# Writing out the middle-block loop of four attention layers, with fixed addresses, in a one-core Trainium2 kernel

## The chip, the cores and the metric

The kernel runs on one core of a Trainium2 chip (trn2). The core has five engines that work side by side, each with its own stream of instructions: TensorE (PE, with its weight loads PEld), VectorE (DVE), ScalarE (ACT), GpSimd (POOL) and SyncE (SP), which here only issues transfers. They meet through semaphores: an instruction may wait until a counter has reached a value, and may raise one when it is done. The metric is the device time of one execution in microseconds (us), lower is better.

## The reference, cut to what matters

A float32 network of four layers; each layer is an attention-like step and a feed-forward step, each followed by a residual sum and a layer norm:

```python
x = _layernorm(x + _L0_attn_ref(x, ...))   # x is (4, 512, 128)
x = _layernorm(x + _L0_ffn_ref(x, ...))
x = _layernorm(x + _L1_attn_ref(x, ...))   # 16 heads of 8, not causal
x = _layernorm(x + _L1_ffn_ref(x, ...))    # mixture of 8 experts, and a shared one
x = _layernorm(x + _L2_attn_ref(x, ...))   # 16 heads, causal, rotary
x = _layernorm(x + _L2_ffn_ref(x, ...))    # grouped-query attention, then 8 experts
x = _layernorm(x + _L3_attn_ref(x, ...))   # grouped-query, causal, with a bias by distance
x = _layernorm(x + _L3_ffn_ref(x, ...))
```

Four of these steps hold a softmax attention over 512 positions and 16 heads of width 8. All four are run by one piece of the kernel, with L = 0 for `_L1_attn_ref`, L = 1 for `_L2_attn_ref`, L = 2 for the attention in `_L2_ffn_ref` and L = 3 for `_L3_attn_ref`. In each:

```python
scores = einsum(q, k) * scale           # per head 512 x 512
attn = softmax(where(mask, -inf, scores))
out = einsum(attn, v) @ wo.T
```

## The kernel before, in words

The batch of four sequences is four **blocks** b = 0..3 of 512 tokens. An attention layer takes them in order, and in each block four **groups** g = 0..3 of four heads. One pass over (b, g) is a **unit**, so a layer has 16 units and a block four. In a unit every engine does its own share, written as a function `unit(L, b, g)` in each engine's program:

- PE: in 10 to 16 items i, `score_t` (L1606, with the mask by L1608) forms the transposed scores of this unit, and `score` (L1590, L1593) forms the plain scores of the unit two ahead, whose row maxima are needed; `values` (L1620) multiplies the exponentials by V; `shift_t` (L1631) and `o_t` (L1640) are small transposes.
- ACT: `PT` (L912) is the exponential of each `score_t` bank.
- DVE: the row maxima, by `TENSOR_REDUCE` (L1189) or, for wide causal tiles, by an addition of the mask with a running maximum (L1186).
- POOL: splits the maxima into bfloat16 parts (L706 to L712), and does the square roots of the norms (L619, L621) and parts of the split of Q and K (L684, L687).
- SP: stores the parts of Q and K (`store_parts`, L511 on), loads the stacks of a group (`load_stack`, L525 and L529) and the shift rows (`load_shift`, L536).

Work of other blocks is laid into the units at fixed places. In g = 0 of block b the projections of block b + 1 are made (`prep_pe` L1574 and L1570, `prep_act`, `prep_pool`). In g = 0 to 3 the block before is ended: its output projection in g = 1 (`y_out`, L1510), its norm in g = 1 and 2 on DVE (`post_sum`, `post_norm` L1026, `stats` L1006 and L1009), and its transpose in g = 3. Nothing reorders any of this: the order is the order in which the program is written, engine by engine.

`sequence` decides which of it is a loop. Block 0 and block 3 are written out; blocks 1 and 2 are one loop body of four units, run twice, on each of the five engines:

```python
def sequence(L, unit, Fori):
    for g in range(NG):
        unit(L, 0, g)
    with Fori(1, NB - 1) as b:
        for g in range(NG):
            unit(L, b, g)
    for g in range(NG):
        unit(L, NB - 1, g)
```

In the body b is a register. A semaphore's threshold that depends on b has to be computed in a register by the engine's sequencer (the rows at L226, L1179, L910 and others), and some helpers add a semaphore increment beside such a wait (L591 on POOL, L1185 on DVE, `pe_passed` on PE). A block's place in `XT` (the transposed input) is also computed from b. For the projection of the values, XT stands on the stationary side of the matmul, and there the body uses a copy at a fixed place, `XTS`: ACT copies XT of the next block to it (L855, `xts`, at item 0 of g = 0), and the projection at L1570 reads XTS and waits for that copy. Where b is a plain number, `prep_act` returns at once for `xts`, and L1570 reads XT itself.

Of the kernel before, what the change touches and what calls it, by code (L numbers as in the profile page):

```python
# [28 lines left out]
NB = 4  # L29
# [5 lines left out]
NG = H // GH  # L35
# [193 lines left out]
def build(nc, d):  # L229
    ctx = ExitStack()  # L230
    with ctx:
# [189 lines left out]

        def sequence(L, unit, Fori):

            for g in range(NG):
                unit(L, 0, g)
            with Fori(1, NB - 1) as b:
                for g in range(NG):
                    unit(L, b, g)
            for g in range(NG):
                unit(L, NB - 1, g)  # L430

# [21 lines left out]
        def ends_chain(L):  # L453
            return any(L == c[-1] for c in CHAINS)
# [16 lines left out]
        def _(sp):  # L471
# [67 lines left out]
            def attention_sp(L):  # L539
# [14 lines left out]
                def unit(L, b, g):  # L554
# [8 lines left out]
                    elif g >= 2 and ahead:  # L563
                        load_stack(ahead[0], ahead[1], g - 1)
                sequence(L, unit, sp.Fori)

            attention_sp(0)
            attention_sp(1)

# [13 lines left out]
        def _(pool):  # L583
            g = nc.gpsimd
# [136 lines left out]
            def attention_pool(L):  # L721
# [5 lines left out]
                def unit(L, b, gg):  # L727
# [14 lines left out]
                    if ahead:  # L742
                        shift(*ahead)
                sequence(L, unit, pool.Fori)

# [50 lines left out]
        def _(act):  # L796
# [100 lines left out]
            def attention_act(L):  # L897
# [6 lines left out]
                def unit(L, b, g):  # L904
                    u = U(L, b, g)
                    prev, follow, ahead, prep, end = neighbours(L, b, g)
                    for i, (kt, js) in enumerate(ST_ITEMS[L]):
# [18 lines left out]
                        if L in GATED_BY and is_last(b) and (g, i) == (2, GATES_AT):  # L926
                            gate_exp(GATED_BY[L], 0)
                sequence(L, unit, act.Fori)
                if ends_chain(L):
                    o_out(L, U(L, NB - 1, NG - 1), NG - 1)  # L930

            def gate_exp(p, part):

                act.wait_ge(gm_ready, gate_part(p, part) + 1)
                t = gate_tiles(part)
                a.activation(GE[:, t, :], GL[:, t, :], ACT.Exp).then_inc(ge_ready, 1)
# [64 lines left out]
        def _(dve):  # L1001
# [200 lines left out]
            def attention_dve(L):  # L1202
# [16 lines left out]
                def unit(L, b, g):  # L1219
                    u = U(L, b, g)  # L1220
                    prev, follow, ahead, prep, end = neighbours(L, b, g)
                    for i in range(NI[L]):
# [24 lines left out]
                        if L in GATED_BY and is_last(b):  # L1247
                            if (g, i) == (2, GATES_AT):
                                gates(GATED_BY[L], 0)
                            if GATED_BY[L] == L1_MOE and g == 3 and i in GATES_T_AT:  # L1250
                                gates_out(GATED_BY[L], GATES_T_AT[i], bank[0])
                                gates_out(GATED_BY[L], GATES_T_AT[i], bank[1], True)
                sequence(L, unit, dve.Fori)
                if ends_chain(L):
# [70 lines left out]
            def gates_out(p, b, src, parts=False):  # L1325

                gi = 0 if p == L1_MOE else 1
                dve.wait_ge(gt_ready, (gi * NB + b) * 2 + (2 if parts else 1))
                if parts:
                    v.tensor_copy(blk(RWT, b)[0:PARTS * NGATE, :], src[0:PARTS * NGATE, 0:T // 2].bitcast(BF16)).then_inc(gt_evac, 1)  # L1330
                else:
                    v.tensor_copy(blk(RW9, b), src[0:NGATE, :]).then_inc(gt_evac, 1)
# [158 lines left out]
        def _(pe):  # L1491
# [158 lines left out]
            def attention_pe(L):  # L1650
# [23 lines left out]
                def unit(L, b, g):  # L1674
                    u = U(L, b, g)
                    prev, follow, ahead, prep, end = neighbours(L, b, g)
                    for i in range(NI[L]):
# [27 lines left out]
                        if L in GATED_BY and is_last(b):  # L1705
                            if g == 2 and i in LOGITS_AT:
                                logits(GATED_BY[L], LOGITS_AT[i], bank[5])
                            if GATED_BY[L] == L1_MOE and g == 3 and i in GATES_T_AT:
                                gates_t(GATED_BY[L], GATES_T_AT[i], bank[0])
                                gates_t(GATED_BY[L], GATES_T_AT[i], bank[1], True)  # L1710
                sequence(L, unit, pe.Fori)
                if ends_chain(L):
# [282 lines left out]
```

## Time and profile before

| what | us |
|---|---|
| median of 3 runs | 1387.44 |
| lowest and highest of the 3 | 1387.06, 1394.69 |
| the profiled execution | 1386.62 |
| its span (first to last instruction) | 1384.8 |
| PE busy in the span | 1218.0 (88%) |
| DVE busy | 932.8 (67%) |
| ACT busy | 710.5 (51%) |
| POOL busy | 269.9 (19%) |

The profile is of one execution; what lies around its span is 1.8 us. In its 40 slices PE is busy at 0.8 or more in nearly all of the stretch from 130 us on. The attention layers are at about 136 to 360 us (L = 0), 564 to 930 us (L = 1 and 2, one after the other) and 1136 to 1315 us (L = 3). TensorE's granted clock is at its full level in the loop blocks. Where a time of a block or unit is given, it is from the start of the first L1606 matmul of one to that of the next.

### The profile page before, as it was taken

The page shows a single profiled execution, that of the slowest core. Times are in us where ns is not written, and L with a number is a line of the kernel's source. Part 1 is how long each engine was busy: PE and PEld are TensorE (multiplying, and loading weights), DVE is VectorE, ACT ScalarE, POOL GpSimd, SP SyncE. Part 2 cuts the span into 40 slices and gives each one's busy share as a digit, 9 for nine tenths or more (in the row PEclk, how much of TensorE's full clock was granted, in tenths as well). Part 3 has the DMA queues.
Part 4 walks back from the last instruction along what each step waited for, and adds up shares of the span by engine and source line. Part 5 has one row for each costly group of instructions (what it writes and reads, how often), then busy time and mean ns, then how long its engine had stood idle before and what let it go on. Part 6 is the DMA issues. An engine that isn't in the chain of part 4 may idle for free.

```text
span 1384.8 us, 26785 instructions
## 1 busy us (share of the span) xinstructions
PE 1218.0 (88%) x8190; PEld 650.1 (47%) x8190; DVE 932.8 (67%) x2502; ACT 710.5 (51%) x1300; POOL 269.9 (19%) x557
## 2 busy tenths in 40 slices
PE   3446999999889998999999999999999979999876
PEld 1222233333356655445555555556666535455445
DVE  5877778687455555767778776755554476668676
ACT  2221776777644434566666666663222227666643
POOL 3342211111000012322332332110000211222112
PEclk7557999999999998999999999999999989999988
DMA  7312232310000003323333222100000202221000
GB/s 207 124 65 73 87 90 68 120 35 19 1 1 1 0 1 120 105 66 107 106 98 126 74 78 76 45 4 3 1 0 0 74 12 67 77 81 40 2 1 31
DMA packets 65200, 79.16 MB, mean 57 GB/s; under 512 B 5483, under 2 KB 58068, under 8 KB 64602
## 3 DMA queue, kind: packets, MB, share of 16 engines
q1 hardware_dynamic: 65098, 77.89, 18.1%
q8 instruction: 52, 0.85, 0.3%
q14 instruction: 50, 0.41, 0.1%
HBM read 45.27 MB, written 31.72 MB: 56 GB/s over the span
## 4 chain that ended last, share of the span: by engine, by line
PE 62%; issue 13%; DVE 9%; ACT 4%; DMA 4%; DVEq 3%; POOL 2%; SPq 1%; POOLq 1%; ACTq 0%
PE bank L1606 11%; PE bank L1620 11%; PE bank L1590 9%; PE bank L1772 6%; PE bank L1773 6%; PE bank L1790 5%; PE bank L1574 3%; PE bank L1608 2%; DVE M L1189 2%; DMA KS<-scr_k 2%; PE bank L1640 2%; DVE masked_scores L1186 1%; PE bank L1510 1%; DVE N L1026 1%; PE bank L1570 1%
## 5 line engine op out<-in xcount | busy, mean ns | idle before, releaser
L912 ACT ACTIVATE PT<-bank 128x512 f32<-128x512 f32 (+1 forms) x784 | 427.5, 569 | 246.9 <-PE bank L1608 176.2
L1590 PE MATMUL bank<-KS,QS 125*128 125x512 bf16 (+3 forms) x1024 | 308.6, 329 | 31.5 <-DVE M L1186 12.1
L1606 PE MATMUL bank<-QS,KS 128*128 128x512 bf16 (+3 forms) x1024 | 303.7, 323 | 15.2 <-ACT PT L912 8.0
L1189 DVE TENSOR_REDUCE M<-bank 128x1 f32<-128x512 f32 (+2 forms) x400 | 257.8, 684 | 87.9 <-PE bank L1590 52.2
L1186 DVE CUSTOM_DVE_ANT_0 masked_scores<-bank,maskw 128x384 bf16<-128x384 f32 (+1 forms) x384 | 228.7, 622 | 90.0 <-PE bank L1590 78.8
L1620 PE MATMUL bank<-PT,VA 128*32 128x512 f32 (+3 forms) x2048 | 211.5, 485 | 1.6 <-ACT PT L912 1.0
L1606 PEld LDWEIGHTS bank<-QS,KS 128*128 128x128 bf16 x1024 | 99.3, 98 | 215.5 <-ACT PT L912 152.4
L1590 PEld LDWEIGHTS bank<-KS,QS 125*128 125x128 bf16 x1024 | 100.6, 99 | 109.0 <-DVE M L1189 31.9
L1608 PE MATMUL bank<-identb,maskw 128*128 128x128 bf16 x768 | 147.7, 219 | 0.0
L1790 PEld LDWEIGHTS bank<-MW,PT 128*128 128x128 f32 x864 | 111.7, 193 | 40.8 <-issue 38.2
L1772 PE MATMUL bank<-XT,MW 128*128 128x512 f32 (+1 forms) x232 | 120.7, 602 | 10.1 <-DVE PT L1363 5.9
L1773 PE MATMUL bank<-XT,MW 128*128 128x512 f32 (+1 forms) x232 | 119.4, 596 | 0.0
L1790 PE MATMUL bank<-MW,PT 128*128 128x128 f32 x864 | 112.2, 276 | 1.2 <-DVE PT L1363 1.2
L953 ACT ACTIVATE PT<-bank 128x512 f32<-128x512 f32 x64 | 38.2, 597 | 130.0 <-PE bank L1773 130.0
L1365 DVE TENSOR_TENSOR PT<-bank,PT 128x512 f32<-128x512 f32 x64 | 44.2, 691 | 79.9 <-ACT PT L953 78.6
L1608 PEld LDWEIGHTS bank<-identb,maskw 128*128 128x128 bf16 x768 | 75.3, 98 | 21.4 <-issue 7.0
L706 POOL CAST MS<-M 128x16 bf16<-128x16 f32 x64 | 12.7, 198 | 331.4 <-DVE M L1189 331.4
L1773 PEld LDWEIGHTS bank<-XT,MW 128*128 128x128 f32 x232 | 44.2, 191 | 55.5 <-issue 55.5
L1504 PE MATMUL bank<-ident,N 128*128 128x128 f32 x128 | 24.8, 328 | 50.5 <-DVE N L1026 50.5
L1620 PEld LDWEIGHTS bank<-PT,VA 128*32 128x32 f32 x2048 | 40.3, 108 | 60.2 <-issue 22.6
L1593 PE MATMUL bank<-maskw,identb 128*128 128x128 bf16 x384 | 66.1, 223 | 0.0
L1359 DVE SCALAR_TENSOR_TENSOR PT<-bank,CC,PT 128x512 f32<-128x512 f32 x52 | 39.0, 749 | 37.3 <-ACT PT L948 37.0
(229 smaller groups left out, 1522.6 us busy)
## 6 DMA issues: line engine op xcount, KB each, us to landing
scr_q<-PQ SPq DMA_DIRECT2D x48, 384.0 KB, 3.2
QS<-scr_q SPq DMA_DIRECT2D x64, 288.0 KB
scr_k<-PK SPq DMA_DIRECT2D x24, 384.0 KB, 3.6
KS<-scr_k SPq DMA_DIRECT2D x32, 288.0 KB
QS<-MSB SPq DMA_DIRECT2D x192, 4.0 KB
MW<-in_m_w SPq DMA_DIRECT2D x3, 1024.0 KB, 9.5
MW<-in_m_w SPq DMA_DIRECT2D x3, 832.0 KB
scr_k<-PK SPq DMA_DIRECT2D x24, 96.0 KB, 1.9
```

What stands on the lines that cost most here:

```text
L912: a.activation(PT[kt % 2][:, js[0]:js[-1] + 1, q0:T], tiles(bank[st_bank(L, g, i)][:, 0:w * len(js)], len(js)), ACT.Exp, scale=c["scale"]) ...
L1186: v.tensor_tensor_reduce(masked_scores[S_ORDER[L][i]][:, 0:kl], bank[S_ORDER[L][i]][:, 0:kl], maskw[:, T - kl:T], -1.0, FLT_MAX, ALU.add, ...
L1189: v.tensor_reduce(M[g % 2][:, t * GH + js[0]:t * GH + js[-1] + 1], tiles(bank[S_ORDER[L][i]][:, 0:kl * len(js)], len(js)), AX_X, ALU.max, ...
L1365: v.tensor_tensor(H1[c % NH1[p]], bank[2 + c % 2][:, :], A1[c % 2], ALU.mult).then_inc(h_ready, 1)
L1590: r = mm(s, QS[0:ROWS_SHIFT, g * GH + j, t * P:(t + 1) * P], KS[0:ROWS_SHIFT, kv_slot(L, g, j), 0:kl], start=True, stop=not by_pe)
L1593: r = mm(s[:, kl - P:kl], identb[:, :], maskb[:, :], start=False, stop=True)
L1606: r = mm(s, KS[:, kv_slot(L, g, j), kt * P:(kt + 1) * P], QS[:, g * GH + j, T - w:T], start=True, stop=not causal)
L1608: r = mm(s[:, 0:P], maskb[:, :], identb[:, :], start=False, stop=True)
L1620: r = mm(bank[4][32 * j:32 * (j + 1), q0:T], VA[:, kt, kv_slot(L, g, j), :], PT[kt % 2][:, j, q0:T], start=(kt == 0), stop=(kt == NT - 1))
L1772: mm(bank[c % 2][:, :], MW1[:, c * P:(c + 1) * P], blk(XT, b), start=True, stop=True)
L1773: r = mm(bank[2 + c % 2][:, :], MW3[:, c * P:(c + 1) * P], blk(XT, b), start=True, stop=True)
L1790: r = mm(to[:, i * P:(i + 1) * P], H1[c % NH1[p]][:, i * P:(i + 1) * P], MW2[:, c, :], start=(starts and i == 0), stop=stops, skip_group_c ...
```

## The change

`sequence` no longer takes a loop; it writes all 16 units out, with b a plain number everywhere. The five calls lose their last argument. The rest of the text is as it was, so lines after this place stand 4 lower in the new kernel. By the rules above the register arithmetic, the branches and the extra increments of the body are no longer issued, the copy to XTS is not made, and the projection at L1570 reads XT. The body of four units stands twice in each engine's stream.

```diff
-        def sequence(L, unit, Fori):
-
-            for g in range(NG):
-                unit(L, 0, g)
-            with Fori(1, NB - 1) as b:
+        def sequence(L, unit):
+
+            for b in range(NB):
                 for g in range(NG):
                     unit(L, b, g)
-            for g in range(NG):
-                unit(L, NB - 1, g)
...
-                sequence(L, unit, sp.Fori)
+                sequence(L, unit)
...
-                sequence(L, unit, pool.Fori)
+                sequence(L, unit)
...
-                sequence(L, unit, act.Fori)
+                sequence(L, unit)
...
-                sequence(L, unit, dve.Fori)
+                sequence(L, unit)
...
-                sequence(L, unit, pe.Fori)
+                sequence(L, unit)
```

First place, ACT at the start of the body of L = 0 (block 1, g = 0). PT0 and PT1 are the exponentials, PQ and QF the two copies of the projected Q, REGISTER_ALU and the bare ISA rows are register work. Before:

```order
L912 ACTIVATE PT1<-bank3 128x512
L426 UNCONDITIONAL_BRANCH
L426 ISA
L226 ISA
L912 ACTIVATE PT0<-bank2 128x512
L853 ISA
L226 REGISTER_ALU
L855 ISA
L855 ACTIVATE XTS<-XT 128x512
L910 REGISTER_ALU
L912 ACTIVATE PT0<-bank3 128x512
```

The same place in the changed kernel:

```order
L908 ACTIVATE PT1<-bank3 128x512
L908 ACTIVATE PT0<-bank2 128x512
L908 ACTIVATE PT0<-bank3 128x512
L866 ACTIVATE PQ<-bank6 128x512
L867 ACTIVATE QF<-bank6 128x512
L908 ACTIVATE PT0<-bank2 128x512
```

The exponentials and the two copies of Q keep their order; the copy to XTS and the register rows between them are gone.

Second place, DVE in g = 2 of the body of L = 1, where the norm of the block before stands between the row maxima of the unit two ahead (masked_scores, M). Before:

```order
L1006 BN_STATS ST<-N 128x6 x4
L1009 BN_AGGR MV<-ST 128x2 x4
L1018 TENSOR_TENSOR MS<-MV 128x4
L1020 TENSOR_TENSOR MS<-MS,MV 128x4
L1179 REGISTER_ALU
L1186 ISA masked_scores,M<-bank,maskw 128x384
L1186 ISA M 128x1
L1179 REGISTER_ALU
L1186 ISA masked_scores,M<-bank,maskw 128x384
L1186 ISA M 128x1
```

In the changed kernel:

```order
L1002 BN_STATS ST<-N 128x6 x4
L1005 BN_AGGR MV<-ST 128x2 x4
L1014 TENSOR_TENSOR MS<-MV 128x4
L1016 TENSOR_TENSOR MS<-MS,MV 128x4
L1182 ISA masked_scores,M<-bank,maskw 128x384
L1182 ISA M 128x1
L1182 ISA masked_scores,M<-bank,maskw 128x384
L1182 ISA M 128x1
```

The work is in the same order; the register rows ahead of each maximum are gone.

## Rows read from the trace of the kernel before

**Rows 1.** The page, busy time, share and count of each engine.

```profile
PE 1218.0 (88%) x8190; PEld 650.1 (47%) x8190; DVE 932.8 (67%) x2502; ACT 710.5 (51%) x1300; POOL 269.9 (19%) x557
```

**Rows 2.** Busy time by stretch; loop blocks 1 and 2 of L = 0, 1, 2, 3.

```profile
core 0: us, PE busy (x) PEld busy (x) DVE busy (x) ACT busy (x) POOL busy (x), PEclk, DMA share, GB/s
192.61:312.53 119.92, 114.55 (x632) 38.56 (x633) 90.88 (x173) 86.92 (x165) 21.68 (x54) 1.00 0.25 80
609.17:706.47 97.30, 92.01 (x836) 50.82 (x833) 72.84 (x233) 61.47 (x120) 28.73 (x62) 1.00 0.32 100
800.36:892.43 92.07, 91.86 (x836) 49.70 (x832) 68.41 (x207) 61.13 (x120) 25.84 (x58) 1.00 0.21 66
1179.99:1275.21 95.22, 89.27 (x828) 48.51 (x824) 68.18 (x225) 62.60 (x122) 24.76 (x58) 1.00 0.20 64
```

**Rows 3.** Semaphore and register work that each engine issues at L226.

```profile
L226 PEldq ALU_OP  x642: 32/32/36, 192.8 to 1273.2; - x161
```

**Rows 4.** By stretch, L = 1: g = 2 of block 2, then of block 3.

```profile
685.07:696.29 11.22, 10.05 (x96) 5.25 (x97) 9.80 (x36) 6.63 (x13) 3.14 (x9) 1.00 0.20 54
732.85:743.57 10.72, 9.92 (x101) 5.27 (x97) 9.69 (x36) 6.64 (x13) 2.97 (x9) 1.00 0.12 38
```

**Rows 5.** DVE in time, L = 1, g = 2: block 1 (644 us), block 3 (740 us).

```profile
644.35 0.16 DVE L1020 TENSOR_TENSOR MS<-MS,MV 128x4 f32<-128x4 f32 x1
644.61 0.56 DVE L1186 CUSTOM_DVE_ANT_0 masked_scores<-bank,maskw 128x384 bf16<-128x384 f32 x1
...
740.05 0.16 DVE L1020 TENSOR_TENSOR MS<-MS,MV 128x4 f32<-128x4 f32 x1
740.13 0.55 DVE L1186 CUSTOM_DVE_ANT_0 masked_scores<-bank,maskw 128x384 bf16<-128x384 f32 x1
```

**Rows 6.** PE in time, L = 1, g = 2 of block 2: idle before, and releaser.

```profile
693.48 0.28 PE L1590 MATMUL bank<-KS,QS 125*128 125x256 bf16 x1 [1.17 <-DVE M L1186]
```

**Rows 7.** By stretch, g = 2 of block 1 of L = 3.

```profile
1206.39:1217.52 11.13, 10.20 (x101) 5.21 (x97) 10.05 (x36) 6.63 (x13) 3.65 (x9) 1.00 0.12 36
```

**Rows 8.** By stretch, L = 1: g = 1 of block 2, then of block 3.

```profile
673.96:685.07 11.11, 10.79 (x108) 6.30 (x105) 8.74 (x32) 7.27 (x15) 3.16 (x7) 1.00 0.48 160
722.12:732.85 10.73, 10.73 (x109) 6.27 (x105) 8.79 (x32) 6.86 (x14) 2.58 (x7) 1.00 0.24 65
```

**Rows 9.** By stretch, L = 0: g = 1 of block 1, then of block 3.

```profile
211.00:225.85 14.85, 14.28 (x80) 5.01 (x81) 12.42 (x29) 9.71 (x19) 2.06 (x6) 1.00 0.15 42
326.66:341.33 14.67, 14.22 (x81) 4.75 (x81) 12.32 (x29) 9.71 (x19) 2.05 (x6) 1.00 0.00 1
```

**Rows 10.** By stretch, L = 3, g = 0: block 1, then block 0.

```profile
1179.99:1195.67 15.68, 13.64 (x116) 7.03 (x113) 7.70 (x23) 10.72 (x21) 5.63 (x9) 1.00 0.32 107
1136.28:1150.67 14.39, 12.27 (x96) 5.98 (x96) 7.34 (x21) 9.59 (x18) 5.57 (x9) 1.00 0.30 98
```

**Rows 11.** The copy to XTS at L855, all 8; duration in ns.

```profile
L855 ACT ACTIVATE XTS<-XT x8: 621/621/622, 193.6 to 1228.8; 128x512 f32 x8
```

**Rows 12.** ACT in time, L = 3, block 1, g = 0.

```profile
1181.06 0.62 ACT L855 ACTIVATE XTS<-XT 128x512 f32 x1
1182.02 0.60 ACT L912 ACTIVATE PT<-bank 128x512 f32<-128x512 f32 x1 [0.33 <-PE bank L1608]
```

**Rows 13.** PE in time: g = 0 of block 1 of L = 3 and of L = 1.

```profile
1183.91 0.59 PE L1574 MATMUL bank<-XT,WC 128*32 x1 [0.77 <-ACT QF L871]
...
610.59 0.39 PE L1590 MATMUL bank<-KS,QS 125*128 125x512 bf16 x1 [0.97 <-DMA KS<-scr_k]
```

**Rows 14.** By stretch, L = 0: block 1, then block 2.

```profile
192.61:252.53 59.92, 57.27 (x317) 19.26 (x317) 45.40 (x87) 43.42 (x83) 10.84 (x27) 1.00 0.26 81
252.53:312.53 60.00, 57.27 (x316) 19.30 (x317) 45.49 (x87) 43.51 (x83) 10.84 (x27) 1.00 0.25 79
```

**Rows 15.** DMA queues of 192.6 to 252.5 us: packets, MB, share of 16 engines.

```profile
q1 hardware_dynamic: 4128, 4.77, 25.1%
q8 instruction: 3, 0.05, 0.3%
q14 instruction: 5, 0.04, 0.2%
```

**Rows 16.** DMA queues of 252.5 to 312.5 us, all of them.

```profile
q1 hardware_dynamic: 4128, 4.77, 25.2%
```

**Rows 17.** Branches of the loops on PE; duration in ns.

```profile
L426 PEldq COMPARE_BRANCH  x8: 76/148/227, 251.6 to 1274.1; - x8
```

## The prediction, made before the changed kernel ran

> **What bounds the kernel now.** I read the busy times first: PE is busy 88% of the span [rows 1], so it is the engine to follow, and only stretches in which PE stands idle can pay. Next I cut the span by blocks of the attention layers, since the change touches blocks 1 and 2 of each and nothing else. The reader is to subtract PE's busy time from each stretch [rows 2]: 119.92 - 114.55 = 5.37 us in L = 0, 97.30 - 92.01 = 5.29 in L = 1, 92.07 - 91.86 = 0.21 in L = 2, and 95.22 - 89.27 = 5.95 in L = 3. That is 16.82 us of idle PE in the 404.5 us that the loops take. PE's matmuls are the same in number and shape after the change, so this is all that there is to win in them, 1.2% of the time. Last I compared units in the loop with the same unit written out: blocks 0 and 3 already are what blocks 1 and 2 become, in the same execution and at the same full clock. These twins carry the forecast.
>
> **The register work.** It is removed. On PE alone one line issues 642 register operations of 32 ns [rows 3], 20.5 us of the sequencer's time. It costs nothing as long as the sequencer runs ahead of the array: in L = 2, which has the same kind of body, PE stands idle for 0.21 us in 92 us [rows 2]. So the 20.5 us are cover, not path, and I take nothing for them. They cost where an engine has just been waited for and its next instruction needs a threshold first. The place where this is seen is DVE in g = 2 of L = 1. There the norm of the block before delays the row maxima, and PE waits for them, 1.17 us [rows 6]. In the loop the maximum starts 644.61 - 644.35 = 0.26 us after the last operation of the norm, in the written-out block 740.13 - 740.05 = 0.08 us [rows 5]. That is 0.18 us at one such place, and there are others like it ahead of it.
>
> What the unit gets from all of them is read from the twins:
>
> - L = 1, g = 2: 11.22 us in the loop, 10.72 written out, with idle PE 1.17 and 0.80 [rows 4]. Gain 0.50 us, twice: 1.0. Most of the wait stays, because it is the norm's own work.
> - L = 3, g = 2: 11.13 us with 0.93 idle [rows 7]. Its written-out blocks have no norm at this place or another one, so it has no twin. It is the same body with the same kind of wait as in L = 1, and I take the same 0.50, twice: 1.0. Bounds: nothing, and all of its idle time, 2 x 0.93 = 1.9.
> - L = 1, g = 1: 11.11 against 10.73 [rows 8]. Gain 0.38, twice: 0.8. Block 1 has more idle here than block 2, from the start of the layer, which the change does not touch; I take block 2's difference for both.
> - L = 0, g = 1: 14.85 against 14.67 [rows 9]. Gain 0.18, twice: 0.4.
> - L = 2: nothing, since PE does not wait [rows 2].
>
> **The g = 0 units and the copy.** The copy takes 0.62 us of ACT, eight times [rows 11], 5.0 us in all. In L = 3 it ends at 1181.06 + 0.62 = 1181.68, and ACT's next exponential starts at 1182.02 after 0.33 us of waiting for PE [rows 12]. The cover is PE's own work for that exponential; take it away and the copy would cost up to 0.62 us each, 5.0 us together. The values projection waits for the copy in name, but it comes five items later, when the copy has long been made. What holds PE in g = 0 is other work: in L = 3 the evacuation of Q by ACT (0.77 us), in L = 1 the landing of a stack (0.97 us) [rows 13]. Neither becomes shorter. The test of it is block 0 of L = 3, which has the same projections without the copy and without a loop: it has 14.39 - 12.27 = 2.12 us of idle PE, and loop block 1 has 15.68 - 13.64 = 2.04 [rows 10]. So the copy and the loop together cost nothing that can be seen there. Each g = 0 unit has a few handoffs between POOL, ACT and PE that lose a register operation or two; I take 0.1 us for each of the six units of L = 0, 1 and 3, together 0.6, between 0 and half the difference of a g = 2 unit. What is late next, if DVE and ACT come earlier, is the same transfer or the same evacuation.
>
> **The branches.** PE's take 76 to 227 ns [rows 17], eight in all. They run on the sequencer, ahead of the array: blocks 1 and 2 of L = 0, of which the first ends with the jump back, take 59.92 and 60.00 us [rows 14]. Nothing is taken for them.
>
> **What is added: code.** The body stands twice, and the second copy has to be fetched. The first pass through the body of L = 0 shows what this looks like: 3 packets of instructions on one queue and 5 on the other [rows 15]. On the second pass there are none [rows 16]. Their time is 0.3% of 16 engines over 59.9 us, 2.9 us, and 0.2%, 1.9 us. The pass that fetches takes 59.92 us and the pass that doesn't 60.00 [rows 14], with the same idle PE (2.65 and 2.73). So the fetch lies beside the work, and its price is zero. If that cover were gone, on PE's queue alone, four layers would pay 4 x 2.9 = 11.6 us; with the other queue's, 4 x 4.8 = 19.2.
>
> The Trainium skill (Runtime: NRT & Kernel Launch, instruction fetch mechanics) says that a taken branch whose target is not in the window that the engine holds forces a fetch of the target before execution can go on, and that kernels therefore prefer to be written out. The trace does not agree for this body: the second pass fetches nothing. By that rule the jump back would stall, and removing it would save at least one fetch in each of four layers; by the rows it saves nothing.
>
> **The sum.** 1.0 + 1.0 + 0.8 + 0.4 + 0.6 = 3.8 us. The profiled execution took 1386.62 us, its span of 1384.8 and 1.8 around it; after the change 1386.6 - 3.8 = 1382.8. The median of the runs is 0.8 above the profiled one, so the forecast is 1383.6 us, 0.3% faster. That is within the 1% that a measurement of this kernel can tell from no change.
>
> **The rivals.**
>
> 1. *Small gains, as summed.* 1383.6 us. Chance 0.60.
> 2. *The twins mislead.* Block 3 differs from blocks 1 and 2 in what follows it as well as in being written out, and an idle stretch that closes in one unit can open in the next. Then the register work is hidden everywhere and the time stays: 1387 us, between 1386 and 1388.5. For it: L = 2 and the g = 0 units of L = 3, where loop and written-out code have the same idle time [rows 2, 10]. Chance 0.22.
> 3. *The fetches of the second copy are exposed.* Engines stall at block 2 of each layer because their instructions are not there. It decides if an engine empties what it holds before the next packet lands. In full on both queues 1387.4 + 19.2 = 1406.6 us, slower by 1.4%. On PE's queue alone 1387.4 + 11.6 = 1399; in part some us, slower by less than 1%. For it: more instruction packets will be there, beside up to 25% of DMA share [rows 15]. Against it: the fetching pass is not longer than the other. Chance 0.04 for over 1%, and 0.06 for less.
> 4. *The jump back stalls after all.* If each layer's jump costs PE one fetch, 2.9 / 3 = 1 us, in a form that the stretches do not show, the gain is 4 us more: 1379.6 us. This is what the skill's rule would make of it. Against it: no packet and no idle time at the jump [rows 14, 16]. Chance 0.03.
> 5. *All idle time of the loops goes.* If one thing in the loop, such as POOL's or ACT's waits on registers, were behind every wait, PE would close all 16.8 us: 1387.4 - 16.8 = 1370.6 us, faster by 1.2%. Against it: written-out units keep 0.80 us in g = 2 of L = 1 and 2.12 in g = 0 of L = 3 [rows 4, 10]. Chance 0.05.
>
> **How the numbers follow.** The time is that of the first. Its own range is from no gain on L = 3 and g = 0 (1385.2) to the full idle time of the g = 2 units of L = 3 and twice the rest (about 1380). The range for 8 in 10 takes in the second rival and the fourth with some room for the 0.8 us between median and profile: 1378.5 to 1388.5. The third and fifth, in all 0.15, stand mostly outside. Faster by over 1% is rival 5, 0.05; slower by over 1% is 3 in full, 0.04; within 1% is the rest, 0.91.
>
> **What would show each step.** In the profile after: the copy row is gone and the projection reads XT. Blocks 1 and 2 of L = 2 still take 46.0 us each. In L = 1 the g = 2 units take 10.7 us, with PE still waiting 0.8 us for DVE. The g = 0 units of L = 3 keep about 2 us of idle PE, waiting for the evacuation of Q and K. There are some 12 more packets of PE's instructions and no longer issue gaps beside them. The prediction is wrong if a block of L = 2 changes by over 0.5 us, since no wait of PE is there to be lost, or if idle PE appears at block 2 beside an instruction packet.

## The result, and the profile after

The changed kernel takes 1382.70 us in the median (1380.18 to 1387.88, 20 runs) against 1387.48 (1384.40 to 1394.69, 20 runs) for the kernel before: ratio 0.9969, with an interval of 0.9958 to 0.9979. The forecast was 1383.6. The profiled execution took 1381.19 us, with a span of 1379.4 against 1384.8, so the profile shows 5.4 us less.

Three parts of the page of the changed kernel: the engines (busy time, share, instructions, as [rows 1]) and the two queues that carry instructions (packets, MB, share of 16 engines).

```profile
PE 1200.9 (87%) x8105; PEld 647.8 (47%) x8190; DVE 932.1 (68%) x2502; ACT 705.8 (51%) x1292; POOL 268.3 (19%) x557
...
q8 instruction: 63, 1.03, 0.3%
q14 instruction: 54, 0.44, 0.1%
```

ACT has 8 instructions fewer: the copies to XTS are gone. The kernel before had 52 and 50 packets on the two queues, so 11 and 4 came with the second copies of the bodies. 85 matmuls have no record here (8105 of 8190), so PE's busy time reads low, and I compare lengths of stretches, not idle sums.

Busy time by stretch of the changed kernel: blocks 1 and 2 of L = 0, 1, 2, 3 (as [rows 2]), then single units, which are g = 1 of L = 0 [rows 9], g = 1 of block 2 [rows 8] and g = 2 of block 2 of L = 1 [rows 4], g = 2 of block 1 and g = 3 of block 2 of L = 2, g = 0 [rows 10] and g = 2 [rows 7] of block 1 of L = 3.

```profile
core 0: us, PE busy (x) PEld busy (x) DVE busy (x) ACT busy (x) POOL busy (x), PEclk, DMA share, GB/s
191.58:310.84 119.26, 112.75 (x620) 37.06 (x632) 90.47 (x173) 85.88 (x163) 21.60 (x54) 1.00 0.26 81
607.49:703.65 96.16, 90.13 (x828) 50.76 (x833) 72.57 (x233) 60.55 (x118) 28.64 (x62) 1.00 0.32 101
797.75:890.36 92.61, 90.20 (x828) 49.76 (x832) 68.10 (x207) 59.97 (x118) 25.49 (x58) 1.00 0.22 66
1176.07:1269.71 93.64, 87.49 (x820) 48.66 (x825) 68.15 (x225) 61.53 (x120) 24.68 (x58) 1.00 0.20 66
...
209.79:224.45 14.66, 14.16 (x79) 4.74 (x81) 12.30 (x29) 9.69 (x19) 2.05 (x6) 1.00 0.16 42
671.15:682.72 11.57, 10.63 (x107) 6.27 (x105) 9.20 (x32) 7.12 (x15) 3.13 (x9) 1.00 0.46 157
682.72:693.42 10.70, 9.68 (x95) 5.26 (x96) 9.26 (x35) 6.63 (x13) 2.91 (x8) 1.00 0.20 56
823.48:833.22 9.74, 9.58 (x99) 5.30 (x96) 8.26 (x27) 6.63 (x13) 1.13 (x6) 1.00 0.14 39
878.87:890.36 11.49, 10.19 (x103) 5.70 (x100) 7.13 (x22) 7.09 (x14) 1.04 (x5) 1.00 0.13 36
1176.07:1191.62 15.55, 13.49 (x115) 7.05 (x113) 7.79 (x23) 10.26 (x20) 5.62 (x9) 1.00 0.32 108
1202.34:1212.81 10.47, 9.76 (x99) 5.26 (x97) 9.52 (x35) 6.63 (x13) 3.63 (x9) 1.00 0.13 38
```

Against [rows 2] the loop blocks become 0.66, 1.14 and 1.58 us shorter in L = 0, 1 and 3, and 0.54 us longer in L = 2: together 2.8 us less, where 3.8 were forecast. The other 2.6 us of the span lie in places that the change does not touch; two steps hold most of it, 1.1 us ahead of the first attention and 1.7 us in the stretch from the last unit of L = 2 to L = 3 (210.5 us against 212.2 before). Experiment e12 shows that the second of these comes and goes with the execution.

What the register work did is seen where [rows 5] showed it. DVE of the changed kernel in time, L = 1, g = 2 of block 1:

```profile
641.25 0.16 DVE L1016 TENSOR_TENSOR MS<-MS,MV 128x4 f32<-128x4 f32 x1
641.33 0.55 DVE L1182 CUSTOM_DVE_ANT_0 masked_scores<-bank,maskw 128x384 bf16<-128x384 f32 x1
```

The maximum now starts 0.08 us after the last operation of the norm, as in the written-out block, instead of 0.26.

L = 2 holds two surprises. Its g = 2 units take 9.74 us instead of 10.13, where PE's row showed 0.11 us of idle time before. And g = 3 of block 2 takes 11.49 instead of 10.18, and has a wait that was not there. PE of the changed kernel in time, with its idle time and what ended it:

```profile
880.46 0.39 PE L1586 MATMUL bank<-KS,QS 125*128 125x512 bf16 x1 [1.14 <-DMA KS<-scr_k]
```

PE waits for a stack. Two rows of the DMA traffic of this kernel, from 877.9 to 879.3 us, show what was on the DMA engines while that stack came in (packets, MB, share of 16 engines):

```profile
q1 hardware_dynamic: 128, 0.11, 28.5%
q8 instruction: 1, 0.02, 5.1%
```

One packet of instructions, 0.02 MB, keeps one engine for 0.051 x 16 x 1.4 = 1.1 us. In the trace the semaphore of the stack has made all its steps but one by 879.15 us, and the last comes at 880.41, after the packet (878.02 to 879.17) has left its engine. The kernel before has no such packet there, because this is the second pass through a body whose code it does not fetch again; from 880 to 882.4 us it has only the data queue:

```profile
q1 hardware_dynamic: 364, 0.35, 45.7%
```

So three questions were open: what makes the g = 2 units shorter, and which engine; whether the copy costs anything; and whether the code packets are what takes a part of the gain back.

### The profile page after: what moved, and what is told of

Read it like the earlier page. It is cut to its first block, busy times and chain, and to the rows that moved or that the text cites. A ratio compares the mean times of both kernels' runs of the same rounds, so it can differ in the third digit from the quotient of the medians.

```text
span 1379.4 us, 24326 instructions
## 1 busy us (share of the span) xinstructions
PE 1200.9 (87%) x8105; PEld 647.8 (47%) x8190; DVE 932.1 (68%) x2502; ACT 705.8 (51%) x1292; POOL 268.3 (19%) x557
## 4 chain that ended last, share of the span: by engine, by line
PE 60%; issue 13%; DVE 10%; ACT 5%; DMA 4%; POOL 3%; DVEq 3%; SPq 1%; POOLq 1%; another core or an unknown queue 0%; ACTq 0%
PE bank L1616 10%; PE bank L1602 9%; PE bank L1586 9%; PE bank L1768 6%; PE bank L1769 6%; PE bank L1786 5%; PE bank L1570 3%; PE bank L1604 3%; DMA KS<-scr_k 2%; DVE masked_scores L1182 2%; DVE M L1185 2%; ACT PT L908 1%; PE bank L1636 1%; PE bank L1506 1%; DVE N L1022 1%
## 5 line engine op out<-in xcount | busy, mean ns | idle before, releaser
L1602 PE MATMUL bank<-QS,KS 128*128 128x256 bf16 (+1 forms) x953 | 276.4, 318 | 11.6 <-ACT PT L908 7.9
```

Of the source, the lines that this page charges most:

```text
L1602: r = mm(s, KS[:, kv_slot(L, g, j), kt * P:(kt + 1) * P], QS[:, g * GH + j, T - w:T], start=True, stop=not causal)
```

## The experiments

A unit is written (L, b, g) below. Three of the kernels are the same as another one: one profile has single waits that another does not repeat, and it has to be known which.

**The changed kernel again, twice.** No edit.

> The changed kernel once more, for a second profile of it. Theory A (what differs between the two profiles inside the attention layers comes from the change): the blocks 1 and 2 of L = 0, 1 and 3 take the same times as in the first profile within 0.1 us, and unit g = 3 of block 2 of L = 2 again takes 11.5 us with PE idle 1.1 to 1.3 us, because the packet of code at 878.0 us falls on the transfer of a stack at the same place of the program. Theory B (chance of one execution): that wait is gone or elsewhere, and the unit takes 10.2 us. Time about 1382.7 us under both, 0.3% under the kernel before.

> The changed kernel a third time, to be compared with the copy beside it on the same chip, and for a third profile. Theory A (the copy is free): this and the next run agree within 1 us in the median. The unit g = 3 of block 2 of L = 2 takes 11.0 to 11.6 us again, g = 0 of L = 1 15.6 to 16.2.

Measured: 1382.69 us beside 1390.05, ratio 0.9954 [0.9937, 0.9971], and 1385.85 beside 1388.97, ratio 0.9983 [0.9969, 0.9997]. Three timings of one pair of kernels thus give 0.9969, 0.9954 and 0.9983, further apart than each interval says; the second rests on 6 executions. Differences of 0.2% between two kernels can't be read from the times, and below I read units, which repeat. Blocks 1 and 2 are shorter than before by 3.1 us in the first (119.28 + 96.14 + 92.41 + 93.53 = 401.4 against 404.5) and 2.6 in the second. What repeats to 0.02 us in all three: (0, b, 0), (0, b, 1) and all g = 2 units. What does not: the units of L = 1 around the start of a block, and (2, 2, 3), with 11.49, 11.11 and 11.67 us. The wait behind the last, in the second repetition, PE in time:

```profile
884.44 0.39 PE L1586 MATMUL bank<-KS,QS 125*128 125x512 bf16 x1 [1.33 <-DMA KS<-scr_k]
```

**The copy put back, twice.** The changed kernel, but blocks 2 and 3 make and wait for the copy to XTS as in the loop.

```diff
-                if what == "xts" and isinstance(b, int):
+                if what == "xts" and isinstance(b, int) and b < 2:
...
-                    x = blk(XT, b) if isinstance(b, int) else XTS[:, :]
-                    if not isinstance(b, int):
+                    copied = not isinstance(b, int) or b >= 2
+                    x = XTS[:, :] if copied else blk(XT, b)
+                    if copied:
```

> The changed kernel, all written out, but with the copy to XTS for blocks 2 and 3 of each layer made on ACT and waited for by PE as in the kernel before. Theory A (the copy lies beside PE's work and costs nothing): the time of the changed kernel, within 0.5 us, and g = 0 of blocks 1 and 2 unchanged: 18.2 us in L = 0, 15.4 to 15.6 in L = 3. Rival (the copy was worth something): up to 8 x 0.62 = 5.0 us slower, which is all of the 4.8 us that the change gained.

> The changed kernel with the copy to XTS put back, the same kernel as the one with the copy above, since its median stood 2.7 us above the changed kernel's while its profile agreed with it in every unit. Theory A (the copy is free; the 2.7 us are the scatter of few runs): within 1 us of the changed kernel run beside it. Rival (the copy costs about what the change gained): again 2 to 5 us above it.

Measured: 1385.43 us, ratio 0.9972 [0.9956, 0.9987], and 1384.18 us, 0.9973 [0.9960, 0.9987]. (0, b, 0) takes 18.20 to 18.21 us in both, as without the copy; the g = 0 units of block 2 of L = 3 take 15.35 in both, again as without it. The copy lies beside PE's work, and its removal brings nothing that the units show. The medians alone would not tell: they lie 2.7 us above that of e1, timed beside the first, and 1.7 us under that of e11, timed beside the second, so both missed the margins that were expected (0.5 and 1 us), in opposite directions.

The two kernels are the same, so their profiles also show what differs between two executions. By stretch, from the last unit of L = 2 to L = 3, first of e2:

```profile
922.78:1133.32 210.54, 195.56 (x955) 120.39 (x952) 118.18 (x352) 58.29 (x96) 18.43 (x30) 0.98 0.05 14
```

and of e12:

```profile
924.29:1136.53 212.24, 197.59 (x955) 121.53 (x953) 118.28 (x352) 58.32 (x96) 18.44 (x30) 0.97 0.05 14
```

1.70 us more at a granted clock of 0.97 instead of 0.98, with the same program. This is the difference that the two profiles of before and after have in this stretch, so it is not the change's.

**DVE alone, and all but DVE.** The kernel before with only DVE's program written out, and the changed kernel with only DVE's program looped. `sequence` takes `Fori` again and writes the blocks out where it is None:

```diff
+            if Fori is None:
+                for b in range(NB):
+                    for g in range(NG):
+                        unit(L, b, g)
+                return
...
-                sequence(L, unit, dve.Fori)
+                sequence(L, unit, None)
```

> The kernel before with only DVE's sequence written out; the four other engines keep the loop, and the copy stays. Theory A (the gain is register work of DVE after its drains and waits, for which PE waits in g = 2): the g = 2 units of blocks 1 and 2 go from 11.22 to 10.7 us in L = 1, from 11.12 to 10.5 in L = 3 and from 10.13 to 9.74 in L = 2; about 3 us less in all, 1384.5 us. g = 0 and g = 1 keep their times. Rival (the gain is at PE, ACT or POOL): g = 2 stays at 11.2 and 11.1 us, time 1387.5.

> The kernel before with SP, POOL, ACT and PE written out and DVE alone in its loop. Theory A: the g = 2 units stay at 11.2 us in L = 1 and 11.1 in L = 3, and only the small gains of g = 0 and g = 1 are left, about 1 us: 1386.5 us. Rival: nearly the whole gain of the change, 1383 us, with g = 2 at 10.7 and 10.5 us.

Measured: 1386.21 us, ratio 0.9980 [0.9967, 0.9992], and 1387.43 us, 0.9985 [0.9972, 0.9998]. By stretch, DVE alone written out, (2, 1, 2), (3, 1, 2) and (1, 2, 2):

```profile
827.71:837.45 9.74, 9.58 (x99) 5.30 (x97) 8.27 (x27) 6.63 (x13) 1.45 (x7) 1.00 0.14 39
1206.14:1216.61 10.47, 9.76 (x99) 5.26 (x97) 9.52 (x35) 6.63 (x13) 3.64 (x9) 1.00 0.14 38
686.10:696.81 10.71, 9.69 (x95) 5.26 (x97) 9.44 (x36) 6.63 (x13) 3.14 (x9) 1.00 0.23 55
```

and all but DVE, (2, 1, 2), (3, 1, 2) and (0, 1, 0):

```profile
827.15:837.28 10.13, 9.78 (x99) 5.28 (x96) 8.70 (x27) 6.74 (x13) 1.36 (x7) 1.00 0.15 38
1208.74:1219.88 11.14, 10.05 (x99) 5.21 (x97) 10.06 (x36) 6.74 (x13) 3.62 (x9) 1.00 0.13 36
193.70:211.90 18.20, 16.23 (x86) 5.81 (x89) 11.02 (x19) 13.70 (x27) 5.71 (x9) 1.00 0.48 165
```

The g = 2 gain is DVE's: with DVE alone five of the six units of L = 1 to 3 have the length of the changed kernel, without it all six have that of the kernel before. In L = 2 too the 0.39 us are DVE's. In (0, b, 0) it is the other way round: 18.39 with DVE alone and 18.20 without it. The g = 1 units of L = 0, 14.85 before and 14.66 after, go to 14.76 with DVE alone and 14.77 with the rest.

The sixth unit is (1, 1, 2), and it shows why e3 missed the 3 us that were expected: its profile has 405.4 us in the four pairs of blocks, no less than the 404.5 before. (1, 1, 1) takes 13.03 us instead of 11.68, with PE idle for 2.46 us at its end until the shift rows (QS<-MSB) land. Right behind that idle time, from 638.0 to 641.5 us, the granted clock is 0.51, about the lower of its two levels (1.2 instead of 2.4 GHz), and (1, 1, 2) takes 11.47 us instead of 10.7. No other kernel with DVE written out has this wait at this length, so whether it comes from the edit or from the one execution is not shown. The median of e3 lies 1.7 us above what was expected.

**PE and ACT alone, and POOL alone.** The same two lines of edit, for these engines.

> The kernel before with PE and ACT written out (so without the copy), and SP, POOL and DVE in their loops. Theory A (the 0.18 us of g = 0 in L = 0 and the 0.14 us in L = 3 come from POOL's waits, which carry a register operation and an increment each, between ACT's casts): g = 0 keeps 18.39 us in L = 0 and 15.5 to 15.7 in L = 3, and the g = 2 units keep 11.1 to 11.2. Time about 1387, no gain. Rival (they come from PE's or ACT's own register work): g = 0 takes 18.2 and 15.35 us. Under both the unit g = 3 of block 2 of L = 2 can be longer, since PE fetches code there.

> The kernel before with POOL alone written out. With PE and ACT written out g = 0 of L = 0 took 18.28 us, between 18.39 and 18.21. Theory A (the rest of that gain is POOL's register work between ACT's casts): g = 0 takes 18.30 in L = 0 and the g = 2 units keep 11.2 and 11.1; the time is that of the kernel before within 1 us. Rival: g = 0 keeps 18.39.

Measured: 1387.71 us, ratio 0.9990 [0.9974, 1.0006], and 1387.79 us, 0.9995 [0.9981, 1.0009]: by the times neither differs from before. By stretch (0, 1, 0), with PE and ACT written out:

```profile
192.01:210.29 18.28, 16.23 (x86) 5.81 (x88) 11.06 (x19) 13.70 (x27) 5.72 (x9) 1.00 0.47 164
```

and with POOL alone:

```profile
191.30:209.59 18.29, 16.41 (x86) 5.92 (x88) 10.95 (x19) 14.21 (x28) 5.71 (x9) 1.00 0.48 164
```

Each gives 0.1 of the 0.19 us of this unit. For e5 18.39 or 18.2 us had been expected, and it is the middle between them. The g = 2 units stay at 11.2, 10.1 and 11.1 us in both (one, (1, 2, 2) of e6, at 11.4). What PE and ACT do bring is the wait for the stack. In e5 (2, 2, 3) takes 11.66 us, the longest but one; PE in time:

```profile
887.38 0.39 PE L1595 MATMUL bank<-KS,QS 125*128 125x512 bf16 x1 [1.31 <-DMA KS<-scr_k]
```

In e6, where PE is a loop and fetches nothing there, the unit takes 10.25. In e3, with DVE written out and PE not, it takes 10.58, and there is a short wait of the same kind:

```profile
883.83 0.39 PE L1595 MATMUL bank<-KS,QS 125*128 125x512 bf16 x1 [0.24 <-DMA KS<-scr_k]
```

The shorter g = 2 unit ahead of it is not the cause. SP issues this stack 3.4 to 3.5 us before the start of (2, 2, 3) in all 12 profiles with SP's old order, so PE does not come to it any earlier. And e4, with DVE looped and a g = 2 unit of 10.13 us, still has 11.05 us at (2, 2, 3), with a packet of PE's code in the transfer. What differs is how long the stack takes from its issue to the last step of its semaphore. Without a packet of PE's code in between it is 3.49 us before, 3.65 in e6 and 3.97 in e3. With one it is 4.6 to 5.3 us, in all seven profiles that have one there: the changed kernel three times, the copy twice, e4 and e5. So the wait has two parts, a scatter of the landing by half a microsecond that needs no code, and about 1 us where a code packet comes in between.

A packet in between does not always delay a stack. In (3, 1, 2) of the changed kernel one runs from 2.98 to 4.01 us after the issue, and the stack lands after 3.74 us, as it does without one; in e2, from 2.75 to 3.65, and the landing takes 5.03.

**L = 2 as a loop, all else written out.** The argument of `sequence` is None for L = 0, 1 and 3 and the engine's Fori for L = 2, where the copy is made as before; as L = 2 is then the only layer with copies, the threshold of PE's wait for them is lower.

```diff
-                sequence(L, unit, pe.Fori)
+                sequence(L, unit, None if L in (0, 1, 3) else pe.Fori)
...
-                        pe.wait_ge(xts_ready, b + (2 * L - 1))
+                        pe.wait_ge(xts_ready, b - 1)
```

> L = 0, 1 and 3 written out on all engines, L = 2 left as the loop of the kernel before, with its copy. Theory A (writing out L = 2 gains 2 x 0.39 us in its g = 2 units and loses 0.9 to 1.4 again where a code packet stands ahead of a stack): g = 2 of L = 2 takes 10.13 us, g = 3 of its block 2 takes 10.18 us, since the second pass fetches nothing, and the time is that of the changed kernel within 1 us, or up to 0.6 under it. Rival (most of the gain is in L = 2): about the time of the kernel before.

Measured: 1384.30 us, ratio 0.9969 [0.9953, 0.9984]. (2, b, 2) is back at 10.13 and 10.12, and (2, 2, 3) comes down from 11.49 to 10.69, not to 10.18. PE in time:

```profile
884.02 0.39 PE L1595 MATMUL bank<-KS,QS 125*128 125x512 bf16 x1 [0.34 <-DMA KS<-scr_k]
```

There is no instruction packet from 876 to 886 us, and still 0.34 us of wait. This missed: the stack, issued at the usual 3.4 us before the unit, takes 4.07 us to land instead of 3.49. It can be late by half a microsecond for a reason other than code, and which one stays open.

**The code packet moved.** The changed kernel with 128 waits on a semaphore that has long been raised, at the start of PE's program. They do nothing, and shift the places at which PE's queue fetches.

```diff
+            for _ in range(PAD):
+                pe.wait_ge(pool_const, 1)
```

> The changed kernel with 128 waits on a semaphore that is long at its value put at the start of PE's stream, where PE has nothing to do yet. They do no work; they move the places at which PE's code is fetched by half a packet. Theory A (unit g = 3 of block 2 of L = 2 is longer because a 16 KB packet of PE's code stands on one DMA engine ahead of the last packets of the stack that this unit waits for): the fetch comes some 6 us earlier there, and the unit goes from 11.1 to 11.5 us back to 10.2. A new collision can appear where the moved packets now fall. Rival (the wait comes from something else in the written-out code, such as SP issuing later): the unit keeps 11.1 to 11.5 us. Time within 1.5 us of the changed kernel's 1382.7 under both.

Measured: 1387.39 us, ratio 0.9988 [0.9970, 1.0006], span of the profile 1380.3. By stretch, (2, 0, 0) and (2, 2, 3):

```profile
751.50:767.67 16.17, 15.01 (x119) 7.57 (x116) 9.96 (x26) 9.46 (x19) 7.38 (x11) 1.00 0.72 254
880.60:891.08 10.48, 10.18 (x103) 5.70 (x100) 7.12 (x22) 7.10 (x14) 1.04 (x5) 1.00 0.13 40
```

The wait has moved. At (2, 2, 3) the packet comes at 876.87 us, before the stack is under way, and the unit takes 10.48 instead of 11.49. At (2, 0, 0), which is 15.01 us in every other kernel written out at PE except e5 (15.08), a packet now begins at 750.33 and takes 1.12 us; the last step of the stack comes at 752.90, and the unit takes 16.17. PE in time:

```profile
752.94 0.39 PE L1589 MATMUL bank<-KS,QS 125*128 125x512 bf16 x1 [1.00 <-DMA KS<-scr_k]
```

The same code at another place makes another stack late, so it is the meeting of the two, not the layer or the block. The landing at (2, 2, 3) still takes 4.08 us, as in e10, so 10.48 and not 10.18 us is what is left without the packet. The ratio of this run lies above all three of the changed kernel, while its profiled span, 1380.3, is like theirs (1379.4, 1380.7, 1383.4); why is open.

**The stack taken out of the packet's way.** In g = 2 and 3 SP issues the rows of the shift first, which must wait for the maxima, and the stack behind them. The edit turns the two around, so the stack is on its way about 7 us earlier, and a packet of 1.1 us can't matter. It is made to the changed kernel (e8) and to the kernel before (e9).

```diff
+                    if g >= 2 and ahead:
+                        load_stack(ahead[0], ahead[1], g - 1)
                     if follow:
                         load_shift(*follow)
                     if prep:
                         store_parts(*prep)
                         load_stack(*prep, 0)
-                    elif g >= 2 and ahead:
-                        load_stack(ahead[0], ahead[1], g - 1)
```

> The changed kernel with one step of SP moved: in g = 2 and 3 the stack of the unit two ahead is loaded before the shift rows of the next unit instead of after them. Its condition is then met at the start of the unit, so it is issued some 5 us earlier. Theory A (what the written-out code loses again is the late stack, delayed by code packets): no code packet can make the stack late, g = 0 of L = 1 goes from 15.6 to 16.2 us to 15.0 in three blocks, and g = 3 of block 2 of L = 2 goes to 10.2; about 4 us less than the changed kernel, 1379 us. Rival (SP's order is not what delays it, or the shift rows become late instead): time 1382.7 or more, and g = 1 and g = 3 units of L = 1 get longer.

> The kernel before, with its loops, and the same move of SP's step as in the run above. Theory A: g = 0 of L = 1 goes from 15.7 to 16.0 us to 15.0, with the loop kept; the gain of writing out and the gain of the early stack add up, so this one is about 2.5 us under the kernel before, near 1385, and the kernel above is 4 to 5 us under this one. Rival (they are one gain, had by either): this kernel reaches the time of the one above.

Measured: e8 1375.66 us, ratio 0.9905 [0.9884, 0.9925]; e9 1383.64 us, 0.9964 [0.9948, 0.9981]. SP's queue of the changed kernel in time: the shift (QS<-MSB), then the two loads of the stack (QS<-scr_q, KS<-scr_k).

```profile
873.49 1.80 SPq L532 DMA_DIRECT2D QS<-MSB  x3
875.34 0.47 SPq L521 DMA_DIRECT2D QS<-scr_q  x1
875.84 0.41 SPq L525 DMA_DIRECT2D KS<-scr_k  x1
```

The same in e8, where this unit, (2, 2, 2), starts at 865.92 instead of 869.13:

```profile
864.99 0.32 SPq L521 DMA_DIRECT2D QS<-scr_q  x1
865.35 0.42 SPq L525 DMA_DIRECT2D KS<-scr_k  x1
870.28 1.82 SPq L532 DMA_DIRECT2D QS<-MSB  x3
```

The stack goes out 0.9 us before the unit's start instead of 6.2 after it. By stretch in e8: (1, 1, 0), blocks 1 and 2 of L = 1, block 2 of L = 2, and its (2, 2, 3).

```profile
607.67:622.28 14.61, 14.45 (x119) 8.18 (x117) 10.00 (x26) 9.47 (x19) 7.15 (x11) 1.00 0.39 124
607.67:701.30 93.63, 89.58 (x828) 50.89 (x833) 72.61 (x233) 60.40 (x118) 28.63 (x62) 1.00 0.33 104
840.19:885.84 45.65, 45.02 (x416) 24.89 (x416) 34.08 (x104) 29.93 (x59) 12.69 (x29) 1.00 0.22 67
875.66:885.84 10.18, 10.02 (x103) 5.74 (x100) 7.14 (x22) 6.99 (x14) 0.99 (x5) 1.00 0.13 40
```

PE's code packet is still there, at 873.59 us and 0.95 us long, and costs nothing. L = 2 has its whole gain now, 91.3 us for blocks 1 and 2 against 92.61 and 92.07 before the change. L = 1 gains 2.5 us more, as its g = 0 units no longer wait for the stack (14.6 us instead of 15.6 to 16.4 in the three profiles of the changed kernel). Another 1.8 us come where the same wait goes outside blocks 1 and 2, in g = 3 of block 0 and g = 0 of block 3 of L = 1. About 4 us less than the changed kernel were expected; the spans differ by 6.5. This is the fastest kernel here, 0.95% below the one before, measured in 5 executions. In e9 the g = 0 units of L = 1 are as short:

```profile
606.42:621.02 14.60, 14.44 (x119) 8.17 (x116) 10.03 (x26) 9.81 (x19) 6.91 (x10) 1.00 0.37 124
606.42:703.82 97.40, 91.23 (x828) 51.21 (x833) 72.95 (x233) 61.48 (x120) 28.61 (x62) 0.98 0.31 99
```

The two blocks together are not. Block 2 takes 46.87 us instead of 48.25. Block 1 takes 50.53 instead of 49.05: PE idles 2.71 us for the shift rows at the end of (1, 1, 1), as in e3, and right behind it the granted clock is at its lower level for 3.4 us. So the sum can't be compared, and whether the new order of SP makes the shift rows later at times is not shown; e8, with the same order, waits 0.74 and 0.77 us for them. That the stack stands behind the shift rows is a cost of the kernel before too, 1.1 to 1.4 us in each g = 0 unit of blocks 1 and 2 of L = 1. By the times it is about as large as what the loop costs. e9 came 1.4 us under the 1385 that were expected, and e8 8 us under e9 instead of 4 to 5; with 7 and 5 executions, and block 1 of e9 disturbed, it is not shown that the two gains together are more than their sum.

## Why the prediction was right, and which steps of it were not

The time, the sign and the size came out as forecast, and in the largest terms by the mechanism that was summed: register work between an engine's wait and its next instruction, in a few units. Not all terms came out.

- **L = 1, g = 2: right.** 0.50 forecast twice, 0.52 and 0.51 measured (11.22 to 10.70 and 10.71). e3 and e4 show that it is DVE's register work.
- **L = 3, g = 2: right in kind, undersized.** 0.50 was carried over from L = 1; it is 0.65 (11.12 to 10.47, 11.12 to 10.46), within its bounds of 0 and 0.93.
- **L = 0, g = 1: right.** 0.18 forecast, 0.19 and 0.20 measured (14.85 and 14.86 to 14.66).
- **The g = 0 units: 0.1 each.** L = 0 has 0.18, one half from PE and ACT and one from POOL; L = 3 has 0.13 and 0.14 in the first profile, and up to 0.33 in block 1 in the others. In L = 1 there is no gain to be seen: the two units together are 0.1 us shorter, 0.3 longer and 0.4 longer in the three profiles.
- **L = 1, g = 1: not borne out.** 0.38 twice was forecast, and the two together gave 0.3, 0.7 and 0.3 us. In the first profile that of block 1 moved by -0.71 us and that of block 2 by +0.45. The twin misled here; that block 3's unit follows another g = 0 unit than block 2's does may be why, and was not tried apart. What moves these units is the wait at the unit's end, in most profiles for the shift rows of the next unit (QS<-MSB): 0.89 us in block 1 and 0.32 in block 2 before; 0.41 (released last by DVE's maxima) and 1.00 in the first profile after. It is still there in e8 (0.74 and 0.77), where these units take 11.30 and 11.34 us, so it is not the late stack of g = 0. What sets it is open.
- **L = 2: "nothing, since PE does not wait" failed twice.** The prediction said itself that a block of L = 2 that changes by over 0.5 us would prove it wrong, and block 2 became 0.93 longer (46.03 to 46.96), and block 1 0.39 shorter. The first failure is the g = 2 units, 0.39 us each from DVE's loop, in stretches that showed only 0.1 us of idle PE. The 0.21 us of [rows 2] are what PE's matmul rows leave idle; the wait stands in the rows of its weight loads, below this list.
- **"The fetch lies beside the work, and its price is zero": failed.** It was read from PE's idle time in L = 0, where no engine waits for code and none does after the change. But the code comes over the DMA engines that bring the stacks. It was the wrong layer to read the price from: in L = 0 the pass with packets and the pass without have the same units, in block 2 of L = 2 PE reaches a stack just as it lands. (2, 2, 3) is 0.9 to 1.5 us longer than before in all seven profiles with the packet, and 0.1 to 0.5 us in the four that are edited and have none (e3, e6, e7, e10), so about 1 us of it is the packet's. It was also among the prediction's own signs of failure, idle PE at block 2 beside an instruction packet.
- **The copy and the branches: zero, right** for the copy by e2 and e12. The branches were not tried apart.

The wait that DVE's loop made in L = 2 was in the trace before, in the rows of the weight loads, which the prediction did not read. PEld in L = 2, (2, 1, 2), before, and the sum of this wait over blocks 1 and 2:

```profile
826.64 0.10 PEld L1590 LDWEIGHTS bank<-KS,QS 125*128 125x128 bf16 x1 [0.44 <-DVE M L1189]
827.24 0.10 PEld L1590 LDWEIGHTS bank<-KS,QS 125*128 125x128 bf16 x1 [0.27 <-DVE M L1189]
...
PEld bank L1590 <- DVE M L1189: 1.4, 4, 0.4
```

and after:

```profile
823.71 0.10 PEld L1586 LDWEIGHTS bank<-KS,QS 125*128 125x128 bf16 x1
824.21 0.10 PEld L1586 LDWEIGHTS bank<-KS,QS 125*128 125x128 bf16 x1
```

The first stands 0.55 us behind the unit's start before and 0.23 after, the second 1.15 and 0.73, and the rest of the unit comes 0.38 us earlier. PE's own rows hide most of this, because matmuls of 0.39 us each are recorded 0.22 us apart: a later start shows as idle time only by what the overlap leaves, 0.11 us.

So the sum of 3.8 us was 2.6 to 3.1 in the three profiles. Gains that were not forecast (0.8 in L = 2, 0.4 or more in L = 3) stand against the late stack (about 1.2, not all of it the packet's) and what L = 1 did not give (about 0.9). That the median of the 20 runs came within 1 us of the forecast is in part owed to these cancelling, and to the scatter of the timings, 0.9954 to 0.9983.

Of the rivals, small gains was the case. The second is not borne out: the g = 2 units keep their gain, and the wait at (2, 2, 3) is not theirs; whether idle time moved from unit to unit in L = 1 is not shown. The third was true in kind, in another form than it was put: not an engine that lacks its instructions, but a data transfer held up. At about 1 us it did not decide. The fourth fell: the unit that ended with the first jump back, (0, 1, 3), took 13.51 us before and 13.60 written out, and what the pass of 59.9 us lost, 0.3 us, lies in its g = 0 and g = 1 units.

The Trainium skill (Runtime: NRT & Kernel Launch, instruction fetch mechanics) says that a sequencer fetches its code in blocks over a DMA queue of its own while it executes the block at hand, and that the cost of this is mostly hidden. The trace agrees as far as issuing goes: block 2 of L = 0, whose second copy is fetched, takes 59.63 us and block 1 59.64. What the fetch does to other transfers, about 1 us at (2, 2, 3), is named in no sentence there; it is read from the rows here.

What is open: why a stack without a packet takes 3.5 us to land in one execution and 4.1 in another; why some packets in a transfer delay it and some do not; the median of e7; and what sets the waits for the shift rows in L = 1.

## What to carry to other kernels

A loop with register arithmetic costs where an engine has just been released and computes the threshold of its next wait, here 0.4 to 0.65 us in a unit of 11 us on the one engine that others wait for, and mostly 0.2 us or less in the other units that changed. Where PE reads as busy, look at the waits of its weight loads too before calling a unit full. Before a price of zero is given to added code, look for the transfers that are waited for within a microsecond of their landing, since a code packet can hold them up by about 1 us. And where such a transfer is found, look at what stands ahead of it in its queue: turning two issues around gave 0.4% on the kernel before (e9) and 0.6% on the changed one (0.9905 against 0.9969), about as much as writing out the loops did or more.

## What the hardware showed that was not expected

A packet of PE's instructions is 16384 bytes and keeps one DMA engine for about 1 us in these traces (0.88 to 1.56 us over the 63 of the changed kernel, 1.15 at 878.0 us). A stack moves in many small packets, and PE waits for the last step of its semaphore; with a code packet in between, that one step came 1.26 us behind all the others, at 880.41 instead of 879.15. That the step is the one of the engine that held the code packet fits this and the price of about 1 us, but no row names the engine. PE's rows can read as full in a unit that loses 0.39 us to a wait, which the rows of its weight loads show. And the stretch between L = 2 and L = 3 takes 210.5 or 212.2 us in executions of the same kernel, at a granted clock of 0.98 or 0.97. In e3 and e9 the granted clock was at its lower level for about 3.4 us right after PE had idled 2.46 and 2.71 us.
